# A two-layer transformer kernel: the first MLP products of a block wait for one PSUM bank instead of for all four down products

## What is computed

```python
# layer 0
x = res + ctx @ Wo.T
h = ada_rms(x, time_emb, ln2_w, ln2_tw)
x = x + jax.nn.silu(h @ Wg.T) * (h @ Wu.T) @ Wd.T
# layer 1
x = x + attn(_ln(x) * (scale1 + 1.0) + shift1) * gamma1
h = _gelu_tanh((_ln(x) * (scale2 + 1.0) + shift2) @ Wfc1.T + bfc1)
x = x + (h @ Wfc2.T + bfc2) * gamma2
```

## Time and profile before

| quantity | value |
|---|---|
| median of 3 runs | 2703.53 us |
| the profiled execution, its own time | 2702.99 us |
| its span (first to last instruction) | 2701.0 us |
| PE busy | 2539.2 us, 94% of the span |
| DVE, POOL, ACT busy | 51%, 39%, 35% |
| mean granted TensorE clock | 0.974 |
| chain that ended last: PE, "issue", DVE, POOL, ACT | 73%, 10%, 7%, 5%, 4% |
| span of a layer 1 block (distance of two last L1500) | 147.5 us |

### The profile page before, as it was taken

One profiled execution on the slowest core, in us unless ns is written; L12 is line 12 of the kernel. 1 busy time (PEld: TensorE's weight loads), 2 busy tenths in 40 slices (PEclk: granted clock), 3 DMA queues, 4 the chain that ended last, 5 costly groups with the idle time before them and its releaser, 6 DMA issues.

```text
span 2701.0 us, 47110 instructions
## 1 busy us (share of the span) xinstructions
PE 2539.2 (94%) x18448; PEld 1268.9 (47%) x18448; DVE 1378.7 (51%) x2138; ACT 947.1 (35%) x1546; POOL 1041.3 (39%) x1007
## 2 busy tenths in 40 slices
PE   6699999999999999999996689999999999999998
PEld 5344444444544444454443345454545445454543
DVE  5455253442524435243245657575857576675741
ACT  3343132231313223132132354453626263534542
POOL 1223232222313223132113456564656556555632
PEclk8899999999999999999997799999999999999999
DMA  5520101001010010100222101212120212121110
GB/s 191 166 81 5 49 3 40 15 5 49 3 51 3 15 38 3 50 3 18 65 103 96 44 21 47 65 29 84 29 76 25 73 40 56 41 58 55 34 54 28
DMA packets 112788, 129.00 MB, mean 48 GB/s; under 512 B 51662, under 2 KB 53966, under 8 KB 112596
## 3 DMA queue, kind: packets, MB, share of 16 engines
q1 hardware_dynamic: 112596, 126.07, 15.6%
HBM read 71.63 MB, written 18.74 MB: 33 GB/s over the span
## 4 chain that ended last, share of the span: by engine, by line
PE 73%; issue 10%; DVE 7%; POOL 5%; ACT 4%; DMA 0%; POOLq 0%; SPq 0%; DVEq 0%; ACTq 0%
PE ps_m L1525 37%; PE ps_abef L1525 18%; PE ps_d L1525 3%; PE ps_c L1525 2%; PE ps_abef L1713 2%; PE ps_abef L1715 2%; PE ps_abef L1720 2%; PE ps_abef L1747 1%; PE ps_d L1701 1%; POOL h_mlp L875 1%; POOL inner L897 1%; DVE weights L1211 1%; PE ps_c L1566 1%; ACT weights L987 1%; POOL scratch L928 1%
## 5 line engine op out<-in xcount | busy, mean ns | idle before, releaser
L1525 PE MATMUL ps_m<-h_mlp,weights 128*128 128x512 f16 x3072 | 707.3, 382 | 40.1 <-POOL h_mlp L875 19.1
L1525 PE MATMUL ps_m<-weights,inner 128*128 128x512 f16 x3072 | 690.4, 379 | 8.7 <-DVE scratch L1365 8.7
L1525 PEld LDWEIGHTS ps_m<-h_mlp,weights 128*128 128x128 f16 x3072 | 296.3, 98 | 385.7 <-issue 37.7
L1525 PEld LDWEIGHTS ps_m<-weights,inner 128*128 128x128 f16 x3072 | 296.8, 98 | 346.2 <-DVE scratch L1365 6.5
L897 POOL TENSOR_TENSOR inner<-scratch,inner 128x512 f16<-128x512 f32 x256 | 301.1, 1176 | 320.7 <-ACT inner L1064 320.7
L1525 PE MATMUL ps_abef<-h_mlp,weights 128*128 128x512 f16 x1536 | 345.4, 379 | 0.4 <-DVE scratch L1365 0.4
L1525 PEld LDWEIGHTS ps_abef<-h_mlp,weights 128*128 128x128 f16 x1536 | 147.6, 98 | 173.8 <-DVE scratch L1365 1.3
L1064 ACT CAST inner<-scratch 128x512 f16<-128x512 f32 x256 | 156.6, 612 | 106.2 <-DVE scratch L1493 68.1
L866 POOL TENSOR_TENSOR scratch<-scratch 128x1 f32<-128x1 f32 x128 | 30.1, 235 | 360.2 <-ACT scratch L1006 304.7
L875 POOL TENSOR_TENSOR h_mlp<-scratch,h_mlp 128x512 f16<-128x512 f32 x64 | 74.0, 1156 | 207.1 <-ACT h_mlp L1021 207.1
L1363 DVE SCALAR_TENSOR_TENSOR scratch<-scratch,ps_m 128x512 f32<-128x512 f32 x64 | 44.0, 687 | 187.7 <-ACT scratch L1076 187.7
(11 more groups left out here) (167 smaller groups left out, 3676.3 us busy)
## 6 DMA issues: line engine op xcount, KB each, us to landing
x_mlp<-x_attn SPq DMA_DIRECT2D x64, 256.0 KB, 2.3
weights<-gamma SPq DMA_DIRECT2D x128, 128.0 KB, 3.0
scratch<-scratch SPq DMA_DIRECT2D x128, 128.0 KB, 2.7
x_attn<-x SPq DMA_DIRECT2D x32, 256.0 KB, 2.7
x_mid<-x_mlp SPq DMA_DIRECT2D x32, 256.0 KB, 2.1
x_attn<-x_mid SPq DMA_DIRECT2D x32, 256.0 KB, 2.8
out<-x_mlp SPq DMA_DIRECT2D x32, 256.0 KB, 2.2
inner<-wada_t SPq DMA_DIRECT2D x4, 1024.0 KB, 6.4
```

Of the source, the lines that this page charges most:

```text
L1525: ins = nc.tensor.matmul(o, left(a, k), right(b, k), start=(first and n == 0), stop=(last and n == len(order) - 1), skip_group_check=True)
```

## The change

The first product of a block now waits for three of the four evacuations, which is the last one of bank 0. The wait for the fourth, on bank 1, stands ahead of the first product that writes this bank: `up` 0 in layer 0, `up` 1 in layer 1. In layer 0 the wait ahead of `gate` 1, which writes neither bank, is gone. Block 0 has no wait at all there. Nothing else differs.

```diff
                             if j >= 2:
                                 pe.wait_ge(L0.m32, it * IC + j - 1)
-                            else:
-                                pe.wait_ge(L0.y, tile(it, 0))
+                            elif j == 0 and not first_block(it):
+                                pe.wait_ge(L0.y, tile(it, 0) - 1)
...
                             w, bank = (gate_w, ps_m[2 * (j % 2)]) if kind == "gate" else (up_w, ps_m[2 * (j % 2) + 1])
+                            if kind == "up" and j == 0 and not first_block(it):
+                                pe.wait_ge(L0.y, tile(it, 0))
                             ins = products([(bank[:], lambda b, k: h_mlp[:, b, k, :])],
...
                             if j >= 2:
                                 pe.wait_ge(L1.u, it * IC + j - 1)
-                            else:
-                                pe.wait_ge(L1.d_g, tile(it, 0))
+                            elif not first_block(it):
+                                pe.wait_ge(L1.d_g, tile(it, j) - 1)
```

## The result

The changed kernel takes 2695.89 us (median of 15 runs, 2688.57 to 2701.05), the kernel before 2702.67 (15 runs, 2696.04 to 2707.62). The ratio is 0.9971, with a 95% interval of 0.996 to 0.9983: by the ratio 7.8 us faster, between 4.6 and 10.8; the two medians lie 6.8 us apart. The forecast was 2696.7, which is 6.8 us under the median it started from.

The account below looks back on a forecast made before the run. PE's instruction list was taken to bound the kernel; 7.7 us of layer 1 gaps less 0.9 for branches plus 0 for layer 0 gave 6.8 us off, 2703.53 to 2696.7 us, range 2695.0 to 2699.8 (8 in 10).

Parts of the forecast that it names:

- What bounds the kernel: Whole kernel: PE, busy 94% of the span, is the clock; a change is worth what it takes from gaps between matmuls.
- Layer 0: nothing: Layer 0 block starts: PE still waits for POOL's `h_lo`, 1.28 us after the removed wait; 0, bounds minus 0.2 to plus 0.2 us.
- Layer 1: 7.7 us of gaps: Layer 1, seven block starts: PE's wait for DVE goes, 6.6 us idle plus 7 x 0.16, together 7.7 us.
- The branch: 0.9 us: Five layer 1 loop starts: the taken branch on PE's sequencer delays the first product, costing 0.9 us; bounds 0 to 5.5.
- D - 3.5: Layer 1 loop starts: a taken branch lasting D us leaves a gap of about D - 3.5 us before the first product.
- R1: Rival, layer 1: code behind the branch comes late, five loop starts gain nothing, only 2.2 us gained, 2701.4 us; chance 0.10.
- Nothing else is next: Rest of the layer 1 block: other waits move along or keep slacks of 1.3 and 1.4 us, costing 0.
- R2: Rival, layer 1 blocks: another wait, such as transposes on DVE or ACT on POOL, replaces each gap; 2703.5 us; chance 0.08.
- R3: Rival, slower: shifted code needs a second fetch at each taken branch in both layers, 17 us slower, 2721 us; chance 0.04.
- what a measurement can tell: Whole kernel: 0.2%, 5.4 us, can be told from no change; the forecast lies above it, so faster got 0.78.
- The range: Whole kernel time, 8 in 10: 2695.0 to 2699.8 us, from branch lengths, 0.7 us for medians, and some widening.
- The clock: no change: Layer 1: clock at its full level in the whole stretch and PE rests less, so no change of it expected.

Follow-up runs that it names:

- experiment 3: The changed kernel with TensorE's six layer 1 loop turns written out, so no branch there; 2696.22 us, ratio 0.997 to the kernel before.
- experiment 2: The kernel before with only the layer 0 half of the change, layer 1 keeping its old wait; 2704.0 us, ratio 0.9998 to before.
- experiment 6: The kernel before with only the layer 1 half, plus layer 0's last-tile statistics and norm a slot earlier; 2677.6 us, ratio 0.9901 to before.
- experiments 5: The changed kernel with statistics and norm of layer 0's last tile one slot earlier; 2675.41 us, ratio 0.9901 to the kernel before.
- experiment 4: The kernel before with layer 1's first two products of a block waiting for POOL's addition of all four down tiles; 2721.97 us, ratio 1.006.
- experiment 1: The kernel before with only the layer 1 half of the change, layer 0 waiting as before; 2697.21 us, ratio 0.9971 to before.
- experiment 7: The changed kernel with layer 0's last-tile norm a slot earlier and both PE loops written out; 2672.01 us, ratio 0.9887 to before.

## Why the prediction came out as it did

**What bounds the kernel.** Right for gaps of up to 1.1 us, which is all that the change touches. They go to the end one to one, shown by the changed kernel (6.8 us in the layer 1 part for the 6.8 forecast) and by experiment 3.

**Layer 0: nothing.** Right, and for the reason given: experiment 2 has no effect, and experiment 6 shows the same wait with its full 0.9 us as soon as `h_lo` no longer ends later.

**Layer 1: 7.7 us of gaps.** Right in place and size. All seven waits are gone.

**The branch: 0.9 us.** Right. It was the term that could not be seen before, because a wait lay over it; the length of the branch could be read, and D - 3.5 came out within 0.02 us at four of the five starts and 0.08 short at the other (0.23 for 0.31); together 1.1 us measured. R1 is refuted: the product follows 0.27 to 0.34 us behind the branch's end where a gap is left, 0.28 in the forecast.

The Trainium skill ("Runtime: NRT & Kernel Launch", section "Instruction fetch mechanics") says that a taken branch to a target outside the current window is held until that target is fetched by DMA. The traces agree: one instruction transfer of 0.9 to 1.8 us lies in each taken branch, none in the ones not taken.

**Nothing else is next.** Right; R2 is refuted by the unchanged list of PE's waits. R3 did not happen, but the 3.3 to 3.9 us that I took as the whole range is not it: in experiments 5 and 6 the loop of layer 0 has branches of up to 4.20 us, with one fetch each that takes up to 1.8 us, where it took 0.9 to 1.4 in the kernel before. No branch in any trace has a second fetch. Why a fetch takes longer at one time than at another is open.

**The step that failed is what a measurement can tell.** The prediction says: "What a measurement can tell from no change is 0.2%, 5.4 us. The forecast lies above it, so faster 0.78", and for the spread it puts "0.7 us for how far medians move, by the runs before", that is, from three runs that lay within 1.6 us of each other. Fifteen runs of the same kernel lie within 11.6 us, and the gain comes out with 3 us to either side: 4.6 to 10.8. A gain of 6.8 us with 3 us on either side begins at 3.7, under 5.4, so even with the mechanism right the step from the sum to 0.78 for a gain that can be told from 0.2% did not follow. What the runs show is that the changed kernel is faster, but not that it is so by more than 0.2%.

The range suffers from the same term. By its own figures (gaps of 7.7 less 0 to 1.8, with 0.7 either way) the gain is 5.2 to 8.4 us and the time 2695.1 to 2698.3, not 2695.3 to 2698.5; its low gain was already under 5.4. The measured median is 0.9 us above the lower end of 2695.0 to 2699.8, while single runs lie from 6.4 us under that end to 1.3 us over the upper one, and the profiled execution, 2700.34 us, lies over it too. The median missed the forecast by 0.8 us because the median of 15 runs of before is 0.9 us under that of three. That the two medians differ by just the 6.8 us of the sum is in part luck, given 3 us on either side; the 6.8 us of the layer 1 part are not. The profile before gave a sign of the spread that I passed over: the granted clock is under 1 in the first slices and again between the layers, and there the traces differ.

**The clock: no change.** True at these seven places, where gaps of 1.1 us left the clock alone before. As an argument it was too weak: I gave the mean of 1.00 in one block as the reason, and did not look at what the 2.7 us gaps of layer 0 do, of which two are followed by a stretch at half clock in the trace of before.

## What to carry to other kernels

When a wait is removed, look at what the engine's own sequencer does under it: a taken branch of 3.3 to 4.2 us was hidden behind 17 queued matmuls and a 1 us wait, and the part that exceeds the queue shows as soon as the wait goes. Before narrowing a wait, find out which wait at that place ends last: in layer 0 the same edit was worth nothing until the norm of the last tile was moved, and that move was worth about three times the whole change (20.7 us). Compare two executions behind a fixed instruction, not by their spans, when their start-ups run at different clocks.

## What the runs showed of the hardware that I had not expected

- A gap of some 2.4 us (2.1 to 2.5) between matmuls is followed by matmuls at half clock at some starts and not at others: five of seven in experiment 4 (24 matmuls in 6.9 to 7.0 us in place of 5.35), and two of seven gaps of 2.7 us in layer 0 before, the same two in seven traces. A gap of 0.9 to 1.2 us at the start of a block was never followed by it in these traces.
- In the last block, behind a wait of 3.1 us for ACT, there is a stretch at half clock in five of the ten traces (in experiment 1, 11 matmuls in 4.90 us) and none in the others (21 in 4.69). In experiment 1 the last block is 2.8 us longer by it.
- A taken branch on PE's sequencer lasts 3.3 to 4.2 us, the one that is not taken 0.08. Each taken one holds one 16 KB transfer of instructions, and it ends 1.2 to 1.5 us after the transfer does.
- Six turns of the layer 1 loop in straight code on PE, and both loops in experiment 7, leave no "issue" gap at the starts of the blocks.
